# A state-space scan inside a two-layer decoder: nine of sixteen states turned instead of eight, on other places in the round

## The reference, cut to what matters

```python
def step(h, inp):
    u_t, dt_t, B_t, C_t = inp
    dA = jnp.exp(jnp.clip(dt_t[..., None] * A, -20.0, 0.0))
    dB_u = jnp.clip(dt_t[..., None] * B_t[:, None, :] * u_t[..., None], -10.0, 10.0)
    h = jnp.clip(h * dA + dB_u, -100.0, 100.0)
    y = jnp.einsum('bds,bs->bd', h, C_t)
    return (h, y)
```

## Time and profile before

| | before |
|---|---|
| median of three runs | 4825.65 us |
| the profiled execution | 4825.39 us, of which the span 4823.6 us |
| scan stage | about 2528 to 3955 us of the span |
| VectorE busy in the stage | 1378.35 us of 1427 |
| GpSimd | 1337.54 us |
| ScalarE | 1184.74 us |
| TensorE matmul | 1175.02 us |

### The profile page before, as it was taken

The page is one execution under the profiler, slowest core; times in us unless marked ns, Lnnn a source line. Parts: engine busy times, 40 slices in busy tenths (PEclk is TensorE's granted clock), DMA queues, the critical chain, the costliest instruction groups (busy, mean ns, idle before and its releaser), DMA issues. The chain is left out here.

```text
span 4823.6 us, 50258 instructions
## 1 busy us (share of the span) xinstructions
PE 4067.3 (84%) x15984; PEld 2334.5 (48%) x15992; DVE 3419.0 (71%) x3827; ACT 2407.7 (50%) x4734; POOL 2588.6 (54%) x1527
## 2 busy tenths in 40 slices
PE   8998986799999549989947888888888878988887
PEld 6776875444444214433314555555455543445544
DVE  5555338522277555538978999999999978955777
ACT  1211114422255641118757888888888865433333
POOL 4444966100033011108878999999999976622221
PEclk9999997599999769989968999999999999999999
DMA  3323226232278765534444233242251127720000
GB/s 110 97 86 86 84 73 195 96 103 96 93 275 298 281 267 198 199 107 176 177 178 153 67 126 106 73 146 81 73 175 62 63 74 261 262 73 18 32 30 35
DMA packets 363929, 625.71 MB, mean 130 GB/s; under 512 B 67238, under 2 KB 152647, under 8 KB 351634
## 3 DMA queue, kind: packets, MB, share of 16 engines
q1 hardware_dynamic: 325506, 578.92, 34.5%
q10 hardware_dynamic: 38160, 43.56, 2.5%
HBM read 394.24 MB, written 228.15 MB: 129 GB/s over the span
## 5 line engine op out<-in xcount | busy, mean ns | idle before, releaser
L2315 POOL TENSOR_TENSOR sc_X<-sc_Bm,sc_w 128x1024 f32<-128x1024 f32 x512 | 1192.5, 2368 | 87.8 <-DVE sc_H L2494 65.7
L1375 PE MATMUL ff_ps<-ffn_R,hand_w 128*128 128x512 f32 x1536 | 662.5, 594 | 0.7 <-ACT ffn_R L1414 0.7
L2337 ACT ACTIVATE sc_A<-sc_dt,keep_A 128x1024 f32<-128x1024 f32 x512 | 581.7, 1136 | 83.9 <-DVE sc_Z L2499 63.1
L2367 ACT ACTIVATE sc_hT<-sc_tp,sc_ct 128x128 f32<-128x128 f32 x2048 | 584.5, 375 | 76.4 <-PE sc_tp L2421 73.6
L2421 PE MATMUL sc_tp<-sc_idn,sc_H 128*128 128x128 f32 x2048 | 316.3, 277 | 223.2 <-issue 144.8
L2442 PE MATMUL sc_yp<-sc_Z,sc_idn 128*128 128x512 f32 x1024 | 489.9, 601 | 9.9 <-ACT sc_yo L2373 9.6
L1375 PEld LDWEIGHTS ff_ps<-ffn_R,hand_w 128*128 128x128 f32 x1536 | 292.0, 191 | 365.8 <-issue 363.7
L2421 PEld LDWEIGHTS sc_tp<-sc_idn,sc_H 128*128 128x128 f32 x2048 | 233.3, 141 | 438.0 <-issue 246.5
L2494 DVE TENSOR_TENSOR_SCAN sc_H<-sc_A,sc_X 128x1024 f32<-128x1024 f32 x160 | 359.0, 2274 | 28.8 <-ACT sc_A L2337 17.4
L2494 DVE TENSOR_TENSOR_SCAN sc_H<-sc_A,sc_hc,sc_X 128x1024 f32<-128x1024 f32 x160 | 368.4, 2336 | 2.3 <-ACT sc_A L2337 2.3
L75 POOL TENSOR_TENSOR gp_pbd<-gp_r,ssm_msk 128x512 f32<-128x512 f32 x144 | 182.0, 1264 | 237.4 <-DVE gp_r L478 237.4
(11 more groups left out here) (423 smaller groups left out, 8122.3 us busy)
## 6 DMA issues: line engine op xcount, KB each, us to landing
sc_Bm<-d_xd SPq DMA_DIRECT2D x64, 512.0 KB, 7.5
ffn_gate_d<-ff_o SPq DMA_DIRECT2D x96, 256.0 KB, 2.3
ffn_up_d<-ff_o SPq DMA_DIRECT2D x96, 256.0 KB, 6.2
ffn_g_d<-ff_z SPq DMA_DIRECT2D x24, 1024.0 KB, 6.4
ffn_R<-ffn_up_d SPq DMA_DIRECT2D x22, 1024.0 KB, 13.3
ffn_R<-ffn_g_d SPq DMA_DIRECT2D x19, 1024.0 KB, 10.4
hand_x<-d_x SPq DMA_DIRECT2D x16, 1024.0 KB, 7.2
ff_g<-ffn_gate_d SPq DMA_DIRECT2D x16, 1024.0 KB, 6.1
```

The source lines that it names most:

```text
L1375: last = nc.tensor.matmul(ps[:, 2 + t % 6], w[:, k, h * P:(h + 1) * P], xt[:, n, k], start=(k == 0), stop=(k == KD - 1))
L2315: nc.gpsimd.tensor_tensor(X[:, k % RX], Bm[:, n], w[:, j % 2], ALU.mult).then_inc(db, 1)
L2337: nc.scalar.activation(A[:, k % 2], dt[:, j % 2], ACT.Exp, scale=keepA[:, n:n + 1]).then_inc(ex, 1)
L2367: nc.scalar.activation(hT[:, turned(k) % 2, q], tp[:, b * P:(b + 1) * P], ACT.Copy, scale=ct[:, i % 2, q, n:n + 1]).then_inc(tc, 1)
```

## The change

The sets of states change, one more state is turned and one less is VectorE's own; the ring `sc_H` has six buffers instead of five; within a step the second half of the older state now stands ahead of the first half of the younger one, on both engines (states 2 and 3, and 9 and 10, are now neighbours, so that a step has two halves); GpSimd's loop runs three steps longer, since the product of state 13 of the last block falls behind the last unit.

```diff
-ON_POOL = (5, 11)
-ON_PE = (0, 2, 4, 6, 8, 10, 12, 14)
+ON_POOL = (6, 13)
+ON_PE = (0, 2, 3, 5, 7, 9, 10, 12, 14)
 LATE = 3
...
-    RX, RZ, RH = 4, 4, 5
+    RX, RZ, RH = 4, 4, 6
...
-            for k in range(NU_):
-                products(k)
+            for k in range(NU_ + 3):
+                if k < NU_:
+                    products(k)
                 if k >= 3 and on_pool((k - 3) % NS):
                     outputs(k - 3)
...
# ScalarE's loop
+                if on_pe((k - 2) % NS) and k > 1:
+                    turn(k - 2, 1)
                 if on_pe((k - 1) % NS) and k > 0:
                     turn(k - 1, 0)
-                if on_pe((k - 2) % NS) and k > 1:
-                    turn(k - 2, 1)
...
# TensorE's loop
+                if 1 < k <= NU_ + 1 and on_pe((k - 2) % NS):
+                    turn(k - 2, 1)
                 if 0 < k <= NU_ and on_pe((k - 1) % NS):
                     turn(k - 1, 0)
-                if 1 < k <= NU_ + 1 and on_pe((k - 2) % NS):
-                    turn(k - 2, 1)
```

## The result

The changed kernel takes 4949.53 us (median of 4 runs, 4944.9 to 4954.01); the kernel before, beside it, 4825.02 us. The ratio is 1.0259 with a 95% interval from 1.0243 to 1.0274: slower by 124.5 us. The forecast was 4928 us, 103 more, in a range of 4871 to 4955.

A forecast was written before the change was run, and what follows sets the result against it. It took the TensorE and ScalarE ring on sc_tp as the bound: 16 x 3.5 + 16 x 2.9 = 103 us, first block -2 and boundaries +2, on 4825.4 gave 4928 us, range 4871 to 4955.

The forecast's parts named there:

- The ring of TensorE and ScalarE: Scan stage: handing the one sc_tp tile to and fro sets the pace, 47.1 us a block against VectorE's 41.45.
- 4785 us by occupancy alone: Rival, scan stage: VectorE stays the bound and the removed work saves 40 us, giving 4785; chance 0.08.
- The double steps: Steps 4 and 11: ScalarE takes out two halves, 1.89 us apart, ahead of the decay for state 7 or 14.
- the clock: Rival, TensorE: granted clock at the lower level a tenth of the time, +2.4 us a block, 5005 us; chance 0.04.
- 47.1 and 46.5: Block lengths in us from the ring's sum: chunks 0 and 2 (+3.5), chunks 1 and 3 (+2.9).
- the two hand-overs: Steps 4 and 11: sc_tp passes between two halves, 1.25 us to TensorE's next half, 0.64 to ScalarE's taking it out.
- The waits' places: VectorE waits for decays: about 2.2 us ahead of state 14, 3.4 ahead of 5, 7 and 15, mostly 7.
- Work on TensorE, six buffers, GpSimd's longer loop at nothing: Small parts of the change: TensorE +0.07 us a block, buffers nothing, GpSimd's last product 0 to 2.4 us, taken as 0.
- The three boundaries: Chunk boundaries: TensorE's lateness passes on in full instead of in part, +2 us.
- The first block: Start of the scan stage: the block is filling anyway, so 2 us less than its share.
- a second loop: Kernel before: the TensorE and ScalarE ring on sc_tp already runs almost as long as VectorE's work.
- 4948, the upper bound: Hand-over price: at most 0.6 us a block more, where the turned half also meets GpSimd's row late.

The follow-up runs named there:

- e7: Changed kernel with second pair at 11 and 12, first halves of states 3, 5 and 12 in the gate's PSUM tile: 4865.92 us.
- e4: Changed kernel with idle TensorE products filling the gaps of step 4: 4930.25 us, 19.3 less than the changed kernel.
- e1: Kernel before with only six row buffers and the new order of the halves: 4825.03 us against 4824.66, ratio 1.000.
- e8: Kernel before with the first halves of states 4 and 12 in the gate's PSUM tile: 4818.35 us against 4822.98, ratio 0.9991.
- e9: Changed kernel with state 10 given back to VectorE, idle TensorE products in steps 4, 14 and 15: 4893.79 us, ratio 1.0139.
- e5: Changed kernel with state 10 given back to VectorE, idle TensorE products in step 4 only: 4933.75 us.
- e11: Changed kernel with the decay buffer of the even units in SBUF and one sc_tp tile: 5311.98 us (2 runs).
- e3: Changed kernel with sc_tp as two tiles in two PSUM banks, the even units' decay buffer moved to SBUF: 5305.59 us, ratio 1.0997.

## Why the prediction was right, and where it was off

- *What bounds.* The ring of TensorE and ScalarE, not VectorE: right. VectorE's busy time fell by 29 us in the stage and the time rose by 124. (Forecast were 39: the product by C alone did fall by 39.2, from 235.1 to 195.9 us, and the rest is mostly that an instruction that follows a wait doesn't overlap the one before.) What the profile showed, 97% of VectorE, would have given 4785 us by occupancy alone.
- *The double steps.* Right, to the instruction: 1.25 and 0.66 us of hand-over in the trace, the wait ahead of 7 and 14. With the clock held at 1.00 the blocks were 47.17 and 46.58 us for 47.1 and 46.5. How this loss divides is shown in part: by e7 some 1.8 us a block are the two hand-overs; the rest of the 3.6 and 3.0 is in the sum, but no run isolates it.
- *The waits' places.* The forecast had 2.2 us ahead of state 14 and 3.4 ahead of 5, 7 and 15 together. Measured in one block of chunk 0: 2.76 ahead of 14, and 0.45 + 2.29 + 0.36 = 3.1. Of the 0.56 too much ahead of 14 the clock explains all: in e4 the wait there is 2.20.
- *Work on TensorE, six buffers, GpSimd's longer loop at nothing.* e1 shows the buffers and the order at 0. The other two were not tested alone; the blocks at full clock come out within 0.1 us of a sum that gives them nothing.
- *The term that failed* is the clock. The forecast gave it as a rival of its own (0.04), for a tenth of the time and 77 us, and left it out of the sum. It is no alternative to the ring but comes with it: in most blocks (23 of the 27 common ones) the gaps of step 4 are followed by some 3 us at half clock, and the 27 together are 18.7 us longer than those of e4, in which the gaps are filled and the clock stays; the median falls by 19.3. That is nearly all of the 21 us between 4928 and 4949.5. The forecast's argument against the clock, a busy share that falls only from 82% to 77% (79% measured), looked at the mean of the stage; what counted was the few us behind the gaps.
- *The three boundaries* cost 3.4, 3.9 and 3.4 us more than the block ahead of them, against 3.2, 2.8 and 3.2 before: 1.5 in all, where 2 were forecast. The first block is 0.7 us longer than before, where the forecast had its share of 3.5 less 2, so 1.5. Both are small.
- *A reading that was too strong.* "Already before the change a second loop runs almost as long as VectorE's" is not shown for the hand-over: e8 gained 5 us instead of 14, and nearly all of that at the chunk boundaries.

The forecast lies 21 us below the median. That the median is inside the range is partly luck: it lies 1.5 us above 4948, the upper bound that the forecast worked out for its sum, and only the 7 us added for the boundaries take it in, while what carried it there was the clock.

## What to carry to other kernels

When two engines pass one buffer to and fro, add up the loop of their hand-overs for a whole round before believing the occupancies: here one engine was 97% busy, both partners had 17% to spare, and two more passes through the buffer, with the clock that fell behind them, cost 2.6% of the program. Taking 40 us of work off the busiest engine pays only if what is added elsewhere doesn't lie on such a loop. And where a change opens gaps on TensorE, price the instructions behind the gaps at half the clock as a term of the sum, then look in the trace at which places it falls: filling gaps helped only where the clock fell behind them.

## What the runs showed of the hardware

- TensorE's granted clock fell to 0.50 behind stretches in which it had only short turns with gaps of 1.3 to 1.6 us between them, although it was busy for some 80% of the block; in four of the 27 common blocks the same steps did not bring it down. With idle products in these gaps it stayed at 1.00 (e4, e9), and a kernel with more instructions was faster. Fills in step 4 left the falls at a block's start as they were (e5).
- A scan on VectorE with both tensors in SBUF takes 2.29 us while GpSimd stands, and beside a busy GpSimd 3.11 in the mean of chunks 0 and 2 and 3.80 in 1 and 3 (e11); with one of them in PSUM it takes 2.27 and 2.33. GpSimd's own product goes from 2.37 to 3.35. The Trainium skill, "SBUF — State Buffer", Who interferes with whom, says that a VectorE instruction with two SBUF inputs contends with a GpSimd instruction that reads SBUF. The trace agrees, for the scan by the numbers above and for VectorE's product (3.19 us from `sc_Ae` in e3, 1.225 from PSUM).
